# Routing one slot later, the attention denominators in slot 3, and y copied earlier in the last group

## What is computed

```python
# attention, 16 heads of 8: q, k through exp, sums over the tokens so far
q = exp(split(x @ Wq.T + bq)); k = exp(split(x @ Wk.T + bk)); v = split(x @ Wv.T + bv)
kv  = cumsum(k[:, :, :, None] * v[:, :, None, :], axis=1)
k1  = cumsum(k, axis=1)
out = einsum('zsD,zsDd->zsd', q, kv) / sum(q * k1, axis=-1)      # num / den
x   = layernorm(x + merge(out) @ Wo.T + bo)

# router: 32 experts in 4 groups, 2 groups and then 8 experts kept for a token
scores = sigmoid(x @ gate_w.T); choice = scores + gate_bias
keep the 2 groups with the largest sum of their top two; keep the top 8 experts of these
weight = scores of the kept / their sum * 2.5

# 32 experts of 64 units and one shared expert of 128 units, all computed for all tokens
y = sum_e weight[e] * ((silu(x @ gate[e].T) * (x @ up[e].T)) @ down[e].T) + shared(x)
x = layernorm(x + y)
```

## Time and profile before

| | |
|---|---|
| median of 3 runs | 454.15 us (451.9 to 813.19) |
| the profiled execution | 450.73 us |
| its span, first to last instruction | 448.9 us |
| PE busy | 425.8 us, 95% of the span |
| DVE, POOL, ACT busy | 76%, 67%, 61% |
| mean granted TensorE clock | 0.994 |
| HBM | 99 GB/s over the span |

### The profile page before, as it was taken

The page is one execution under the profiler, slowest core; times in us unless marked ns, Lnnn a source line. Parts: engine busy times, 40 slices in busy tenths (PEclk is TensorE's granted clock), DMA queues, the critical chain, the costliest instruction groups (busy, mean ns, idle before and its releaser), DMA issues.

```text
span 448.9 us, 10927 instructions
## 1 busy us (share of the span) xinstructions
PE 425.8 (95%) x4000; PEld 327.6 (73%) x4000; DVE 340.7 (76%) x905; ACT 275.6 (61%) x536; POOL 302.6 (67%) x225
## 2 busy tenths in 40 slices
PE   7888999999999999999999999999999999989992
PEld 5766877778777887778776887778777786666771
DVE  3767896896778697796878777886967968768644
ACT  4755558744887359754696358863697447554642
POOL 3554668836967578855878369664878467777791
PEclk9999999999999999999999999999999999999997
DMA  8400845255234545045354544245461542237400
GB/s 284 171 1 21 195 100 119 61 116 129 75 77 101 118 96 140 26 107 131 75 117 101 115 100 96 54 95 118 95 142 50 120 104 70 66 98 177 112 20 23
DMA packets 28885, 45.10 MB, mean 100 GB/s; under 512 B 2080, under 2 KB 10656, under 8 KB 28448
## 3 DMA queue, kind: packets, MB, share of 16 engines
q1 hardware_dynamic: 28544, 44.14, 41.1%
q10 hardware_dynamic: 288, 0.26, 0.2%
HBM read 41.77 MB, written 2.62 MB: 99 GB/s over the span
## 4 chain that ended last, share of the span: by engine, by line
DVE 34%; PE 31%; POOL 14%; issue 11%; ACT 3%; DVEq 1%; ACTq 0%; POOLq 0%
PE bank L379 29%; POOL units L1136 9%; DVE units L979 8%; POOL hidden_lo L1176 3%; DVE hidden_lo L846 3%; DVE stats L866 3%; DVE top_of_group L907 2%; DVE bank L900 2%; DVE x L878 2%; DVE probs L856 2%; ACT hidden_hi L697 2%; DVE replaced L939 1%; DVE out_sb L1043 1%; DVE bank L1061 1%; DVE mean_var L871 1%
## 5 line engine op out<-in xcount | busy, mean ns | idle before, releaser
L1136 POOL TENSOR_TENSOR units<-units,weight_wide 128x512 f32<-128x512 f32 x127 | 175.7, 1389 | 101.6 <-DVE units L979 92.3
L697 ACT ACTIVATE hidden_hi<-units 128x512 fp32r<-128x512 f32 x136 | 85.8, 632 | 65.5 <-POOL units L1136 62.2
L979 DVE TENSOR_TENSOR units<-bank,units 128x512 f32<-128x512 f32 x136 | 92.3, 683 | 32.3 <-PE bank L379 21.2
L716 ACT ACTIVATE units<-bank 128x512 f32<-128x512 f32 x136 | 80.1, 590 | 57.8 <-PE bank L379 57.2
L846 DVE TENSOR_TENSOR hidden_lo<-units,hidden_hi 128x512 fp32r<-128x512 f32 x103 | 90.8, 883 | 23.6 <-ACT hidden_hi L697 23.5
L379 PE MATMUL bank<-x_hi,gate_hi 128*128 128x512 f32 x136 | 61.1, 450 | 1.2 <-ACT units L716 0.5
L379 PE MATMUL bank<-x_hi,up_hi 128*128 128x512 f32 x136 | 56.1, 412 | 2.6 <-ACT units L716 2.6
L379 PE MATMUL bank<-hidden_hi,down_hi 128*128 128x512 f32 x136 | 54.5, 400 | 2.3 <-POOL hidden_lo L1176 1.9
L379 PE MATMUL bank<-x_lo,gate_hi 128*128 128x512 f32 x136 | 53.9, 397 | 0.0
L379 PE MATMUL bank<-x_hi,gate_lo 128*128 128x512 f32 x136 | 53.9, 396 | 0.0
L379 PE MATMUL bank<-x_hi,up_lo 128*128 128x512 f32 x136 | 53.8, 396 | 0.0
(11 more groups left out here) (129 smaller groups left out, 694.5 us busy)
## 6 DMA issues: line engine op xcount, KB each, us to landing
weight_wide<-weight_d SPq DMA_DIRECT2D x60, 512.0 KB, 6.7
x_tok<-x_in SPq DMA_DIRECT2D x8, 256.0 KB, 6.8
xT<-xT_in SPq DMA_DIRECT2D x7, 256.0 KB, 6.7
out_dram<-out_sb SPq DMA_DIRECT2D x7, 256.0 KB, 2.3
weight_wide<-up_in SPq DMA_DIRECT2D x1, 1088.0 KB, 6.8
up_raw<-up_in SPq DMA_DIRECT2D x1, 1088.0 KB, 8.9
down_raw<-down_in SPq DMA_DIRECT2D x1, 1088.0 KB, 7.8
weight_wide<-weight_d SPq DMA_DIRECT2D x8, 128.0 KB, 3.1
```

What stands on the lines that cost most here:

```text
L697: nc.scalar.activation(hidden_hi[place(n, g)][:, :], units[place(n, g)][:, :], ACT.Copy).then_inc(hidden_hi_done, 1)
L716: nc.scalar.activation(units[place(n, g)][:, :], banks[up_bank(2 * n, g)][:, :], ACT.Silu).then_inc(silu_done, 1)
L979: V.tensor_tensor(units[place(n, g)][:, :], banks[up_bank(2 * n + 1, g)][:, :], units[place(n, g)][:, :], ALU.mult).then_inc(gated_done, 1)
L1136: G.tensor_tensor(units[place(n, g)][:, :], units[place(n, g)][:, :], weight_wide[:, w % (2 * PIECE), :], ALU.mult).then_inc(hidden_done, 1)
```

## The change

Five things are moved; no arithmetic is added or taken away.

1. For groups m = 1 to 6 the three pieces of the router on DVE run in slots 11, 12 and 13 instead of 10, 11 and 12. PE turns the weights in slot 15, after that slot's gate and up products, instead of at the end of slot 14, and ACT copies them in slot 15. (Group 7 had its turn and copy in slot 15 already, and keeps its router slots.)
2. For m = 2 to 7 PE sums the denominators in slot 3 instead of slot 0, ACT copies them at the end of slot 3, and DVE takes the reciprocal in slot 3 instead of 2. The turn of y in slot 4 now waits for ACT's copy, as they share a bank, and the second scores no longer do.
3. For f = 2 to 7 DVE scans k at the end of slot 0 of the following group instead of in slot 14, and reads k alone (before, the second, unused operand was a piece of a PSUM bank).
4. POOL multiplies with q in slot 1 of the following group, instead of slot 15.
5. In the last group ACT copies y in slot 3, ahead of the rounding of block 2, instead of at the start of slot 4.

```diff
--- before.py
+++ after.py
@@ -452,7 +452,8 @@
                 else:
                     pe.wait_ge(kv_copied, SEQS * (f + 1))
                     pe.wait_ge(weightT_copied, f)
-                    pe.wait_ge(k_scanned, SEQS * (f + 1))
+                    if f == 1:
+                        pe.wait_ge(k_scanned, SEQS * (f + 1))
                 pe.wait_ge(k_exp, reached(f + 1))
                 pe.wait_ge(q_masked, reached(f + 1))
                 scores(f, 0, range(QUADS))
@@ -519,7 +520,7 @@
                     keep_warm(WARM["up"])
                 if ffn:
                     up(n, g, u)
-                if m == GROUPS - 1 and n == 15:
+                if mid and m > 0 and n == 15:
                     turn_weights(m)
                 if tail and 0 < n < LAG:
                     down(BLOCKS - LAG + n, g - 1)
@@ -543,6 +544,7 @@
                     pe.wait_ge(y_copied, reached(t + 1))
                     if mid:
                         pe.wait_ge(probs_done, SEQS * QUADS * m + QUADS + 2)
+                        pe.wait_ge(den_copied, m + 1)
                     for i in range(TILES):
                         if t == GROUPS - 1 and i == TILES // 2:
                             pe.wait_ge(y_copied, GROUPS + 1)
@@ -551,14 +553,14 @@
                                                    yT[:, 128 * i:128 * i + 128], ident)
                         if i == TILES - 1 or t == GROUPS - 1 and i == TILES // 2 - 1:
                             last.then_inc(y_turned, 1)
-                if mid and n == 0:
+                if mid and n == (0 if m < 2 else 3):
                     pe.wait_ge(qk_sum_done, reached(m + 1))
                     if m == 0:
                         pe.wait_ge(kv_copied, SEQS)
                     elif m == 1:
                         pe.wait_ge(gated_done, 2)
                     else:
-                        pe.wait_ge(probs_done, reached(SEQS * QUADS * m + 2))
+                        pe.wait_ge(probs_done, reached(SEQS * QUADS * m + QUADS + 2))
                     for i in range(TILES):
                         last = mm(den_bank(m)[2 * HEADS * i:2 * HEADS * (i + 1), 0:128],
                                   head_ones, k_sum[:, 128 * i:128 * i + 128])
@@ -575,7 +577,6 @@
                         scores(m, 1, (2, 3))
                     else:
                         pe.wait_ge(probs_done, SEQS * QUADS * m + QUADS)
-                        pe.wait_ge(den_copied, m + 1)
                         scores(m, 1, range(QUADS))
                 if mid and n == 2:
                     if m != 1:
@@ -657,7 +658,7 @@
                         last = mm(seq_banks[c % 2][:, at:at + 128], k_tok[rows, i, :], v_tok[rows, i, :])
                         if (b, c) in ((1, 1), (1, 2)):
                             last.then_inc(kv_ready if c == 2 else kv_odd_ready, 1)
-                if mid and n == 14 and m < GROUPS - 1:
+                if m == 0 and mid and n == 14:
                     turn_weights(m)
                 if front and n == 16 and f != 1:
                     first_scores(f)
@@ -697,14 +698,17 @@
                 nc.scalar.activation(hidden_hi[place(n, g)][:, :], units[place(n, g)][:, :], ACT.Copy
                                      ).then_inc(hidden_hi_done, 1)
 
+            def copy_y(t):
+
+                act.wait_ge(down_done, reached(BLOCKS * (t + 1)))
+                act.wait_ge(y_turned, reached(t))
+                for c in (HALVES if t == GROUPS - 1 else (slice(0, GROUP),)):
+                    nc.scalar.activation(yT[:, c], y_bank[:, c], ACT.Copy).then_inc(y_copied, 1)
+
             def slot(n, g, u, ffn, mid, front, tail):
                 m, f = g + 1, g + 2
-                if tail and n == 4:
-                    t = g - 1
-                    act.wait_ge(down_done, reached(BLOCKS * (t + 1)))
-                    act.wait_ge(y_turned, reached(t))
-                    for c in (HALVES if t == GROUPS - 1 else (slice(0, GROUP),)):
-                        nc.scalar.activation(yT[:, c], y_bank[:, c], ACT.Copy).then_inc(y_copied, 1)
+                if tail and n == 4 and g != GROUPS - 1:
+                    copy_y(g - 1)
                 if ffn:
                     act.wait_ge(g_ready, reached(BLOCKS * g + n + 1))
 
@@ -780,20 +784,26 @@
                                 v_tok[64 * odd:64 * odd + 64, 2 * b:2 * b + 2, :].rearrange(
                                     "p i (q j d) -> p (i q) j d", j=2, d=16)[:, :, :, dims], ACT.Copy)
                     last.then_inc(v_spread, 1)
-                if mid and n == (14 if m < GROUPS - 1 else 15):
+                if mid and n == (14 if m == 0 else 15):
                     act.wait_ge(weight_turned, reached(m + 1))
                     act.wait_ge(weight_written, reached(16 * m))
                     nc.scalar.activation(weightT[:, :], mid_banks[1][0:EXPERTS, :], ACT.Copy
                                          ).then_inc(weightT_copied, 1)
                 if tail and n == 0:
                     high_part(BLOCKS - 1, g - 1)
-                if mid and n == 0:
+                if mid and m < 2 and n == 0:
                     act.wait_ge(den_ready, reached(m + 1))
                     act.wait_ge(inv_done, reached(m))
                     nc.scalar.activation(den_cols[:, :], den_bank(m)[:, 0:128], ACT.Copy).then_inc(den_copied, 1)
+                if g == GROUPS - 1 and n == 3:
+                    copy_y(g - 1)
                 if ffn:
                     for b in ready_blocks(n, g):
                         high_part(b, g)
+                if mid and m > 1 and n == 3:
+                    act.wait_ge(den_ready, reached(m + 1))
+                    act.wait_ge(inv_done, reached(m))
+                    nc.scalar.activation(den_cols[:, :], den_bank(m)[:, 0:128], ACT.Copy).then_inc(den_copied, 1)
 
                 if tail and n in OUT_SLOTS and (g < GROUPS or n == OUT_SLOTS[0]):
                     t = g - 1
@@ -969,7 +979,7 @@
                 dve.wait_ge(den_ready, reached(f))
                 for b in range(SEQS):
                     k = kT[:, b * SEQ:(b + 1) * SEQ]
-                    V.tensor_tensor_scan(k_sum[:, b * SEQ:(b + 1) * SEQ], k, k if f < 2 else route[:, 0:SEQ], 0.0, ALU.add, ALU.bypass
+                    V.tensor_tensor_scan(k_sum[:, b * SEQ:(b + 1) * SEQ], k, k, 0.0, ALU.add, ALU.bypass
                                          ).then_inc(k_scanned, 1)
 
             def gating(n, g):
@@ -1032,7 +1042,7 @@
                                     weight_wide[:, 2 * PIECE - 1, :], ALU.mult).then_inc(last_hidden_done, 1)
                 if mid and (0 if m < 2 else 1) <= n < 3:
                     masked_probs(m, 1 + n)
-                if mid and n == (0 if m == 0 else 2):
+                if mid and n == (0 if m == 0 else 2 if m == 1 else 3):
                     dve.wait_ge(den_copied, reached(m + 1))
                     dve.wait_ge(inv_turned, reached(2 * m))
                     V.reciprocal(inv_den[:, :], den_cols[:, :]).then_inc(inv_done, 1)
@@ -1072,7 +1082,7 @@
                         k_totals(1)
                 if front and f > 1 and n == 14:
                     masked_states(f)
-                if front and f != 1 and n == 14:
+                if front and f == 0 and n == 14:
                     k_totals(f)
                 if front and f == 0 and n == 14:
                     rows_bias()
@@ -1086,14 +1096,17 @@
                     masked_probs(f, 0)
                     if f > 1:
                         masked_probs(f, 1)
-                if mid and n == 10:
+                later = 1 if 0 < m < GROUPS - 1 else 0
+                if mid and n == 10 + later:
                     expert_scores(m)
                     group_tops(m)
-                if mid and n == 11:
+                if mid and n == 11 + later:
                     masked_experts(m)
-                if mid and n == 12:
+                if mid and n == 12 + later:
                     expert_weights(m)
                 low_parts(n, g, ffn, tail)
+                if mid and m > 1 and n == 0:
+                    k_totals(m)
 
             schedule(slot)
 
@@ -1166,8 +1179,10 @@
                     pool.wait_ge(u_ready, reached(BLOCKS * (m - 1) + 1))
                     G.tensor_tensor(x1_lo[1 - u][:, :], x1T[:, :], x1_hi[1 - u][:, :].bitcast(F32), ALU.subtract
                                     ).then_inc(x1_lo_done, 1)
-                if front and f != 1 and n == 15:
+                if front and f == 0 and n == 15:
                     q_times_totals(f)
+                if mid and m > 1 and n == 1:
+                    q_times_totals(m)
                 if mid and m == 0 and n == 13:
                     q_times_totals(1)
                 if ffn and n - 1 in pool_lows(g):
```

## The result

The changed kernel takes 460.51 us (median of 4 runs, 458.73 to 462.06), the kernel before 453.02 beside it (median of 4 runs, lowest 451.17; one of them took 813.19 us and is left out of the ratio). The ratio is **1.0188 [1.0131, 1.0244]**: slower, and by an amount that this measurement cannot tell from 2%. The profiled execution took 460.19 with a span of 458.4 us, 9.5 above the 448.9 of before.

The account below looks back on a forecast made before the run. PE, busy 95% of the span, bounds the kernel, so waits add to the end. Terms 12.1 - 2.1 - 0.2 = +9.8 us gave 460.5 by the profiled execution; 462 was set between 460.5 and 464, range 454.5 to 468.

Parts of the forecast that it names:

- Router, +12.1: Groups 0 to 5: router starts 3.52 us later behind block 11's silu, slot 15 covers 1.50; 2.02 each.
- Denominators, -2.1: Leaving slot 0 saves PE 0.85 us, slot 3 costs 0.5: gain 0.35 in each of six groups.
- Scans and product, 0: DVE's scans in slot 0, POOL's product in slot 1: readers many matmuls later, so no cost; up to 1.3 us uncovered.
- Weights to DRAM and back, 0: Reloaded weights land about 199.6, POOL's shifted block 1 wants them about 199.7: a tie, at no cost.
- y in the last group, -0.2: Earlier copy of y removes PE's single 0.4 us wait; counted -0.2 us (0 to -0.4), as the stretch behind awaits weights.
- The 462: Forecast time in us, set between 460.5 (from the profiled execution) and 464.
- PE absorbs the waits: First rival: PE catches up behind its waits, weight loads being 73% busy; +1.6 us, time 451 to 456, chance 0.12.
- the change does what its places suggest: Second rival: block 11's silu does not delay the router, waits go; -4 us, time 446.7 to 450, chance 0.07.
- The second wait beside the first: Third rival: late POOL product and weights hold slot 3's denominators; 1 to 1.3 us more in six groups, 468 to 470, chance 0.11.
- The forecast's observation for the period: Sign named for groups 0 to 5: each group's period grows 1.5 to 1.8 us.

Follow-up runs that it names:

- the pair with one table: Changed kernel and kernel before, each with silu replacing exp for k, q and exp(-T) behind the first group: 447.57 us (ratio 0.9927) and 449.71 us (0.9978).
- the kernel with the router back and the scans behind: Changed kernel with the router's move undone and the scan of k behind slot 1's masked scores: 449.16 us, ratio 0.9953 to the kernel before.
- the kernel with the router alone: Kernel before with only the router, the turn and the copy of its weights moved: 462.08 us, ratio 1.0236.
- With the router back: Changed kernel with only the router's move undone, all the rest kept: 450.31 us, ratio 0.9984 to the kernel before.

## Why the prediction was right, and where its sizes were off

**Router, +12.1: the mechanism as it was put, 0.1 us a group less.** The steps were: gating of block 11 right behind its silu, router 0.61 behind it, same length, turn behind the router's end, a wait of some 1.2 us behind slot 15's six matmuls. All are in the rows above: 4.04 us idle, 0.61, 10.19 us and 1.06. The router starts 8.80 us behind the gate product of block 10 in place of 5.25, 3.55 later against 3.52 forecast; slot 13 is 0.68 longer against 0.65. Slots 12 to 15 cost 12.95 - 11.03 = 1.92 in place of 2.02. The difference is in the turn: it starts 0.05 us behind the router's end, where 0.21 had been taken from the row of before. There PE was itself busy until then: its twelve products for the states take 1.09 us to the next start in the kernel after (188.09 to 189.18), and 184.50 + 1.09 is 185.59. The 0.21 was not the price of the hand-over, but PE's own lateness. The kernel before had the right row, in group 7, whose turn stands in slot 15 and waits for its weights: it starts 0.06 us behind the router's end there. That the cause is silu behind ACT's table load was argued; the pair with one table shows it.

**Denominators, -2.1: too large.** Taking them out of slot 0 saves 2.12 - 1.40 and 3.43 - 3.33, or 0.82 (forecast 0.85). In slot 3 they cost 4.60 - 4.04 = 0.56 (allowed: 0.50). That makes -0.26 a group, which the kernel with the router back and the scans behind shows (slots 0 to 3: 13.37 against 13.63). But with the router late, a part of this is had already: in the kernel with the router alone, slot 0 falls to 1.98, since PE comes later and finds the masked scores ready: its wait before the denominators is 0.06 us, for POOL's product, in place of 0.21. Next to that the move is worth 13.47 - 13.36 = 0.11 in group 2, and 0.05 to 0.12 by the periods of groups 1 to 6, 0.5 in all. Two terms of the sum had the same wait in them, and I added them.

**Scans and product, 0: right here by luck, as the prediction left out the reader that matters.** I named the bank that the gating behind the scans frees, and left out the masked scores of slot 1, which stand behind the scans as well and which PE's attention sums read. With the router back that costs 0.24 us a group, and it used up what the denominators gave. In the changed kernel DVE is far enough ahead there.

**Weights to DRAM and back, 0: right.** POOL's block 1 in group 3 begins at 202.64 behind a gating, not behind the load; the turn and the loads moved together. The forecast called it a tie, and it is one: the second load landed at 202.41. In group 2 POOL did wait for the load, and with the router alone in each of groups 1 to 6; slots 0 to 3 on PE are no longer for it.

```profile
202.64 1.30 POOL L1149 TENSOR_TENSOR units<-units,weight_wide 128x512 f32<-128x512 f32 x1 [4.68 <-DVE units L989]
```

**y in the last group, -0.2: about nothing.** The wait went, and the next one, POOL's for its weights, took its place. I had written that the stretch behind waits for weights too, and still counted half. What the traces give is 0 to -0.6, by when the weights land.

**Sum and time.** Forecast +9.8 in span, measured +9.5 (+9.8 without the work ahead of group 0, which the change does not touch): 12.1 became 10.7 (the router alone: six periods 2.15, 1.77, 1.71, 1.60, 1.82 and 1.68 longer; six times the 1.92 of slots 12 to 15 would be 11.5, less the 0.14 that slot 0 gives back each time), and -2.1 became -0.5 (after's periods of groups 1 to 6 against the router alone). Group 0 with -0.3, for which there was no term and whose cause is open, group 6 with -0.2 (the wait in its slot 0, gone with the router alone too), the last with +0.1 and the start with -0.3 make up the 9.5. The agreement in the sum is thus in part luck: errors of 1.4 and 1.6 that cancel. The 462 was 1.5 above the measured median, since I set it between two ways to count from the span to the median; the sum against the profiled execution's own time, 460.5, was the better of the two. Whether the change costs over 2%, to which the forecast gave 0.53, stays open: 1.88% was measured, and the interval has 2% in it.

**The rivals.** That PE absorbs the waits did not come: its weight loads went from 73% to 71% busy and hid none of the delay. That the change does what its places suggest came only where the table load was taken away: 2.5 us faster in span there, of which 1.5 are in the groups, where up to 4 had been put. The second wait beside the first, at POOL's product and the weights, did not come on PE: the denominators of slot 3 wait for nothing in groups 1 to 6, though in group 2 POOL began block 1 behind the load. The forecast's observation for the period, 1.5 to 1.8 us longer, fits groups 0 to 5 (1.53 to 1.82).

## What to carry to other kernels

An engine that works its list in order has holes where it waits; before a long chain is moved on it, look whether the chain now stands in such a hole. The first piece of the chain fixes its end: moved behind the instruction that the hole waits for, the whole chain is later by the hole, while later pieces of it can move at no cost. Count a wait once even if two parts of a change remove it, and for work put into a slack stretch go through everything queued behind it, not only the nearest reader.

## What the runs showed of the hardware

- A switch of ACT's table costs its load and nothing more that can be seen here: 1.28 us at 179.06, and the next activation starts at 180.35, 0.01 us behind its end; so it is at all 16 loads of the kernel before and all 16 of the kernel after. All of the damage came from what was queued behind it.
- A hand-over from DVE to a waiting PE takes less than a row in which PE is busy suggests: the turn starts 0.05 us behind the end of DVE's last instruction (191.85 to 191.90), and 0.05 to 0.06 us behind it for the weights of groups 1 to 7 in the kernel after.
- After small products PE's first step is longer: 0.34 us from start to start (189.18 to the next gate product at 189.52) behind the states, in place of 0.23. It is 0.31 to 0.34 us behind nearly every group of small products in both kernels. Behind the denominators in slot 3 it falls on the products for the sums, whose first step is 0.27 us there and 0.16 in slot 2: 0.1 of the 0.56 us that they cost.
